# A two-layer AdaLN/FFN kernel: c turned by VectorE in 32x32 blocks, conv moved in front of up's second half

## What is computed

```python
# layer 0
att = softmax(mlp(cond))                                   # (b, 8)
y   = einsum('boi,bih->boh', einsum('bk,koi->boi', att, weight), x) + (att @ bias_k)[:, :, None]
x1  = x + y @ W_up.T + lora_B[e] @ (lora_A[e] @ y) * 1.0   # e = argmax(y @ gate_w.T + expert_bias)
# layer 1
c   = conv1d(x1, weight, 9 taps, pad 4, 4 groups) + (cond @ c_weight.T)[:, :, None] + bias
r   = route(softmax(c @ W_gate.T), top 2, renormalised)    # (tokens, 8 experts)
out = x1 + c @ W_base.T + b_base + einsum('bner,eor->bno', (c @ A.T) * r, B)
```

## Time and profile before

| | before |
|---|---|
| median of 3 runs | 400.89 us (400.55 to 401.44) |
| the profiled execution | 400.67 us |
| its span, first to last instruction | 398.9 us |
| mean granted TensorE clock | 0.996 |
| TensorE busy | 383.5 us, 96% |
| VectorE busy | 270.0 us, 68% |
| ScalarE busy | 103.5 us, 26% |
| GpSimd busy | 160.4 us, 40% |

### The profile page before, as it was taken

How to read it: one execution, slowest core, us unless ns; L and a number is a source line. 1 busy time by engine, 2 the same in 40 slices (tenths; PEclk the granted TensorE clock), 3 DMA queues, 4 the chain that set the end, 5 groups by cost and what they waited for, 6 DMA issues and landing times.

```text
span 398.9 us, 8234 instructions
## 1 busy us (share of the span) xinstructions
PE 383.5 (96%) x2615; PEld 354.9 (89%) x2615; DVE 270.0 (68%) x837; ACT 103.5 (26%) x251; POOL 160.4 (40%) x146
## 2 busy tenths in 40 slices
PE   4999999999999999999999999999999999999995
PEld 2887999989999999999999999999999999999984
DVE  4568667657766676777667767676677676766553
ACT  4733222222122222221222222212222222222211
POOL 4314444243444443334444433344444333444420
PEclk9989999999999999999999999999999999999999
DMA  5803342212122222112222321222222212222111
GB/s 131 268 15 114 116 140 81 80 32 65 64 78 79 79 79 74 37 61 65 79 79 79 79 78 30 63 66 79 79 79 79 58 50 64 66 79 79 54 53 55
DMA packets 31404, 30.75 MB, mean 77 GB/s; under 512 B 4740, under 2 KB 21556, under 8 KB 31392
## 3 DMA queue, kind: packets, MB, share of 16 engines
q1 hardware_dynamic: 31184, 30.19, 26.1%
q0 software_dynamic: 208, 0.41, 0.4%
HBM read 13.79 MB, written 8.40 MB: 56 GB/s over the span
## 4 chain that ended last, share of the span: by engine, by line
PE 86%; issue 2%; DVE 1%; DMA 1%; ACT 1%; SPq 0%; DVEq 0%
PE ps_base L912 18%; PE ps_conv L865 17%; PE ps_up L829 15%; PE ps_base L917 9%; PE ps_up L834 7%; PE ps_mix L789 7%; PE ps_base L883 5%; PE ps_ct L894 4%; PE ps_up L776 2%; PE ps_turn L768 2%; DMA xq<-x1p 1%; PE ps_turn L760 1%; SPq L293 0%; DVE x1p L598 0%; DVE c L680 0%
## 5 line engine op out<-in xcount | busy, mean ns | idle before, releaser
L364 POOL TENSOR_TENSOR y_lo<-y,y_hi 128x512 fp32r<-128x512 f32 x31 | 40.1, 1293 | 198.8 <-ACT y_hi L407 198.8
L912 PE MATMUL ps_base<-base_hi,c_hi 128*128 128x392 f32 (+1 forms) x256 | 77.7, 320 | 1.1 <-ACT c_hi L458 1.1
L912 PE MATMUL ps_base<-base_lo,c_hi 128*128 128x392 f32 (+1 forms) x256 | 75.0, 310 | 0.0
L829 PE MATMUL ps_up<-up_hi,y_hi 128*128 128x292 f32 (+1 forms) x256 | 67.9, 292 | 0.7 <-ACT y_hi L407 0.7
L829 PE MATMUL ps_up<-up_lo,y_hi 128*128 128x292 f32 (+1 forms) x256 | 67.5, 291 | 0.0
L508 DVE TENSOR_TENSOR mix_w<-gsum,quad 128x64 f32<-128x64 f32 x64 | 48.1, 753 | 6.6 <-DVE gl L648 5.3
L371 POOL TENSOR_TENSOR x1b<-x1p,bbase_s 128x512 f32<-128x512 f32 x32 | 50.1, 1566 | 4.1 <-DVE ot L688 4.1
L912 PEld LDWEIGHTS ps_base<-base_hi,c_hi 128*128 128x128 f32 x256 | 48.4, 189 | 1.5 <-DVE ot L688 1.5
L829 PEld LDWEIGHTS ps_up<-up_hi,y_hi 128*128 128x128 f32 x256 | 48.9, 191 | 0.9 <-ACT y_hi L407 0.9
L829 PEld LDWEIGHTS ps_up<-up_lo,y_hi 128*128 128x128 f32 x256 | 48.9, 191 | 0.0
L917 PE MATMUL ps_base<-base_hi,c_lo 128*128 128x392 f32 (+1 forms) x256 | 48.4, 311 | 0.0
(11 more groups left out here) (156 smaller groups left out, 626.7 us busy)
## 6 DMA issues: line engine op xcount, KB each, us to landing
xt<-in_x SPq DMA_DIRECT2D x32, 256.0 KB, 3.0
xq<-x1p SPq DMA_DIRECT2D x128, 64.0 KB, 2.2
out_x<-ot SPq DMA_DIRECT2D x32, 256.0 KB, 3.0
rows<-agg_rows SPq DMA_DIRECT2D x2, 597.0 KB, 4.1
wup_raw<-in_L_ffn_W_up SPq DMA_DIRECT2D x2, 512.0 KB, 5.5
wbase_raw<-in_L_ffn_W_base SPq DMA_DIRECT2D x2, 512.0 KB, 5.2
rows<-agg_rows SPq DMA_DIRECT2D x1, 598.0 KB, 4.7
rows<-agg_rows SPq DMA_DIRECT2D x1, 256.0 KB, 4.0
```

What stands on the lines that cost most here:

```text
L364: pool.tensor_tensor(y_lo[:], y32[:], y_hi[:], ALU.subtract).then_inc(ylo_done, 1)
L829: pe.matmul(into, y_hi[:, k], w[:, k, cols], start=(k == 0 and w is up_hi), stop=False, skip_group_check=True)
L912: pe.matmul(ps_base[:, j, 0:width], c_hi[:, q], w[:, q, j, 0:width], start=(q == 0 and w is base_hi), stop=False, skip_group_check=True)
```

## The change

- c of tile i-1 is evicted from PSUM by ScalarE, one activation (Identity, with the bias as a per-partition operand) for each of the four samples, in place of two adds on VectorE.
- It is turned by two VectorE instructions of 128x256 that transpose 32x32 blocks, SBUF to PSUM, in place of four TensorE transposes. The partitions of the turned c are then (phase, low five bits of the position), so w_base, a1 and w_gate are reordered to match, by GpSimd copies ahead of the fills; w_gate's fill becomes the last one.
- TensorE's order in a middle step becomes: up with the gate's columns, conv's first six products, the turn of hw, conv's last three, up's other columns with the turn of z before its last four products, delta, LoRA product, mix, base.
- On VectorE the output sum is split in two halves of 256 columns, one on either side of x1p; base waits for its own half only.
- Of x1's four transfers SP issues two; ScalarE issues the other two, after c_hi and before y_high of the next tile.

The diff, cut to its core:

```diff
+        base_p, a1_p, g1_p = sb("base_p", [P, KC, H]), sb("a1_p", [P, H]), sb("g1_p", [E1, H])
 ...
-            fills.append(((in_base, 32), [wbase_raw[:, dc, q:H:NQ] for dc in range(KC)], KC, P,
+            fills.append(((basep_ready, KC), [base_p[:, dc, cols] for dc in range(KC)], KC, P,
 ...
@@ sync
-                    for b in range(SPT):
+                    for b in range(SPT // 2):
                         sp.dma_start(xq[:, b, 1:1 + NM], x1p[b * C:(b + 1) * C]).then_inc(xq_in, 16)
@@ gpsimd, before the steps
+            pool.wait_ge(in_base[0], 16)
+            for dc in range(KC // 2):
+                pool.tensor_copy(by_chunk(base_p[:, dc]), chunk_rows(wbase_raw[:, dc])).then_inc(basep_ready, 1)
             pool.wait_ge(y32_done, 1)
             pool.wait_ge(yhi_done, 1)
             pool.tensor_tensor(y_lo[:], y32[:], y_hi[:], ALU.subtract).then_inc(ylo_done, 1)
+            pool.wait_ge(in_base[1], 16)
+            for dc in range(KC // 2, KC):
+                pool.tensor_copy(by_chunk(base_p[:, dc]), chunk_rows(wbase_raw[:, dc])).then_inc(basep_ready, 1)
+            pool.wait_ge(in_a1, 16)
+            pool.tensor_copy(by_chunk(a1_p[:]), chunk_rows(a1_raw[:])).then_inc(a1p_ready, 1)
+            pool.wait_ge(in_gate, 16)
+            pool.tensor_copy(by_chunk(g1_p[:]), chunk_rows(g1_raw[:])).then_inc(g1p_ready, 1)
@@ scalar
+            def conv_out(t):
+
+                act.wait_ge(conv_done, t + 1)
+                after(act, ct_done, t * 2)
+                for b in range(SPT):
+                    act.activation(c32[:, b], ps_conv[:, 0, b * NM:(b + 1) * NM], ACT.Identity,
+                                   bias=biasT[:, bass.ds(t * SPT + b, 1)]).then_inc(c32_done, 1)
 ...
+                if final:
+                    z_high(i)
+                if once(i - 1):
+                    conv_out(i - 1)
 ...
+                if once(i) and not final:
+                    z_high(i)
 ...
-                    act.wait_ge(ct_done, i)
+                    act.wait_ge(ct_done, i * 2)
 ...
+                if once(i):
+
+                    act.wait_ge(x1_done, i + 1)
+                    after(act, xqlo_done, i)
+                    for b in range(SPT // 2, SPT):
+                        act.dma_start(xq[:, b, 1:1 + NM], x1p[b * C:(b + 1) * C]).then_inc(xq_in, 16)
                 if once(i + 1):
                     y_high(i + 1)
@@ vector
+            def turn_c(t):
+
+                after(dve, clo_done, t)
+                for half in range(2):
+                    dve.wait_ge(c32_done, t * SPT + (half + 1) * (SPT // 2))
+                    dve.transpose(ps_ct[:, 0, half * HALF:(half + 1) * HALF],
+                                  c32[:, half * (SPT // 2):(half + 1) * (SPT // 2)].rearrange("p b m -> p (b m)"))\
+                        .then_inc(ct_done, 1)
+
+            def out_sum(i, par, j):
+
+                if j == 0:
+                    dve.wait_ge(delta_done, i - 1)
+                    dve.wait_ge(x1b_done, i - 1)
+                    after(dve, stored[par], pair_count(i, par, -4))
+                dve.tensor_tensor(ot[:, par, j * HALF:(j + 1) * HALF], ps_base[:, j, 0:HALF],
+                                  x1b[:, par, j * HALF:(j + 1) * HALF], ALU.add).then_inc(out_done, 1)
 ...
                 if final:
+                    z_low(i)
                     x1_sum(i, par)
                 if once(i - 1):
-                    dve.wait_ge(conv_done, i)
-                    after(dve, ct_done, i - 1)
-                    for half in range(2):
-                        b2 = slice(half * SPT // 2, (half + 1) * SPT // 2)
-                        dve.tensor_tensor(c32[:, b2], ps_conv[:, 0].rearrange("p (b m) -> p b m", b=SPT)[:, b2],
-                                          biasT[:, bass.ds((i - 1) * SPT + half * (SPT // 2), SPT // 2)].unsqueeze(2)
-                                          .to_broadcast([P, SPT // 2, NM]), ALU.add).then_inc(c32_done, 1)
+                    turn_c(i - 1)
+                if once(i) and not final:
+                    z_low(i)
                 if once(i - 2):
-                    dve.tensor_tensor(ot[:, par].rearrange("p (j d) -> p j d", j=2), ps_base[:, :, 0:HALF],
-                                      x1b[:, par].rearrange("p (j d) -> p j d", j=2), ALU.add)\
-                        .then_inc(out_done, 1)
+                    out_sum(i, par, 0)
                 if once(i) and not final:
                     x1_sum(i, par)
+                if once(i - 2):
+                    out_sum(i, par, 1)
@@ tensor
+            def up_half(t, j, cols, done, between=None):
 ...
+                if j == 1:
+                    pe.wait_ge(ylo_done, t + 1)
+                if between is not None:
+                    between(t)
 ...
                     pe.wait_ge(yhi_done, i + 1)
                     after(pe, x1_done, i)
+                    up_half(i, 1, slice(HALF, L0W), upgate_done)
+                if once(i) and (final or not once(i - 1)):
+                    up_half(i, 0, slice(0, HALF), up_done)
 ...
                     pe.wait_ge(xqhi_done, i)
-                    after(pe, c32_done, (i - 1) * 2)
+                    after(pe, c32_done, (i - 1) * SPT)
                     for part, (rhs, weights) in enumerate(((xq_hi, (conv_hi, conv_lo)), (xq_lo, (conv_hi,)))):
                         if part == 1:
-                            if last:
+                            if once(i - 2) and not final:
                                 turn_hw(i - 2)
                             if final:
                                 lora_delta(i)
-                            elif once(i):
-                                turn_z(i)
                             pe.wait_ge(xqlo_done, i)
 ...
+                elif once(i) and not final:
+                    up_half(i, 0, slice(0, HALF), up_done, turn_z)
 ...
-                    after(pe, clo_done, i - 1)
-                    for b in range(SPT):
-                        if b % (SPT // 2) == 0:
-                            pe.wait_ge(c32_done, (i - 1) * 2 + 1 + b // (SPT // 2))
-                        mm = pe.transpose(ps_ct[:, 0, b * P:(b + 1) * P], c32[:, b], ident[:])
-                    mm.then_inc(ct_done, 1)
 ...
-                    after(pe, out_done, i - 1)
                     for j, width, done in ((0, L1W, basegate_done), (1, HALF, base_done)):
+                        after(pe, out_done, (i - 2) * 2 + 1 + j)
```

More of the change, by code:

```diff
@@ L369, in body @@
                     pool.wait_ge(x1_done, i + 1)
-                    after(pool, out_done, i - 1)
+                    after(pool, out_done, (i - 1) * 2)
                     pool.tensor_tensor(x1b[:, par].rearrange("p (m q) -> p m q", q=NQ),
@@ L575, in _ @@
             y_sum(0)
-            for n in range(3, NF0):
+            for n in range(3, NF1):
                 low_part(n)
@@ L754, in _ @@
                 .then_inc(attb_done, 1)
+            def up_half(t, j, cols, done, between=None):
+                into = ps_up[:, j, 0:cols.stop - cols.start]
+                for k in range(KC):
+                    for w in (up_hi, up_lo):
+                        pe.matmul(into, y_hi[:, k], w[:, k, cols], start=(k == 0 and w is up_hi),
+                                  stop=False, skip_group_check=True)
+                if j == 1:
+                    pe.wait_ge(ylo_done, t + 1)
+                if between is not None:
+                    between(t)
+                for k in range(KC):
+                    mm = pe.matmul(into, y_lo[:, k], up_hi[:, k, cols], start=False,
+                                   stop=(k == KC - 1), skip_group_check=True)
+                mm.then_inc(done, 1)
             def turn_hw(t):
@@ L818, in body @@
             def body(i, par):
+                final = isinstance(i, int) and i == NT - 1
+                last = isinstance(i, int) and i >= NT
                 if once(i):
@@ L822, in body @@
                     after(pe, x1_done, i)
-                    for j, cols, done in ((1, slice(HALF, L0W), upgate_done), (0, slice(0, HALF), up_done)):
-                        into = ps_up[:, j, 0:cols.stop - cols.start]
-                        for k in range(KC):
-                            for w in (up_hi, up_lo):
-                                pe.matmul(into, y_hi[:, k], w[:, k, cols], start=(k == 0 and w is up_hi),
-                                          stop=False, skip_group_check=True)
-                        if j == 1:
-                            pe.wait_ge(ylo_done, i + 1)
-                        for k in range(KC):
-                            mm = pe.matmul(into, y_lo[:, k], up_hi[:, k, cols], start=False,
-                                           stop=(k == KC - 1), skip_group_check=True)
-                        mm.then_inc(done, 1)
+                    up_half(i, 1, slice(HALF, L0W), upgate_done)
+                if once(i) and (final or not once(i - 1)):
+                    up_half(i, 0, slice(0, HALF), up_done)
```

(4 more changed lines are left out.)

56 lines of the change are left out of this document (27 added, 29 removed).

## The result

| | before | after |
|---|---|---|
| median of 13 runs each | 400.19 us (398.64 to 402.14) | 403.54 us (401.25 to 405.14) |
| ratio, 95% interval | | 1.0077 (1.0054 to 1.0101) |
| the profiled execution, its span | 400.67, 398.9 us | 402.86, 401.0 us |
| mean granted clock | 0.996 | 0.996 |
| tile: mean distance of delta's first products, 60 to 340 us | 11.45 us | 11.467 us |

The account below looks back on a forecast made before the run. TensorE's stream was taken as the bound, with about 0.3 us a tile of waits. 29 tiles of 11.0 against 331.57 gave -12.6, start 0, end +0.5: span 386.8, so 388.8 us as median; range 379 to 399.

Parts of the forecast that it names:

- a loop over the output sum, x1p, c_lo, y_hi and GpSimd to conv: Loop setting the tile: 10.96 us by c_lo's arm, 11.04 by GpSimd's; taken as 11.0 against 11.43.
- x1p starts at D+0.54: On VectorE: the first half sum waits until D+0.19, takes 0.35, then x1p starts.
- That chain just fits.: c's evictions, VectorE's transposes and z_low end at about S+2.95, when TensorE wants z_low at the LoRA product.
- The second rival: c's new chain too slow: output sum 0.4 to 0.5 later, tile 11.4, gain gone, 400 us; chance 0.13.
- The third rival: ScalarE's transfer issues hold y_hi up 0.94 if both queues slow each other; tile 11.98, 417 us; chance 0.11.
- S to D: TensorE from conv's last three products to delta's end: 0.83 + 1.41 + 0.71 = 2.95 us.
- the floor: TensorE's stream without waits, 10.64 us a tile; as a rival, c_lo and xq_lo on time, 378.4; chance 0.12.
- 0.32 late: c_lo usable at D+2.60 where TensorE wants to load it at D+2.28, in each tile.
- costed at nothing: mix_w makes zm late, but z's turn moves 0.94 us back in TensorE's stream, so no cost was expected.
- Needed: Splitting x1's transfers over two queues lets xq_hi start near D+4.5; worth 0 to 0.1 us a tile.
- The start: Fills and GpSimd weight copies ahead of the middle tiles: sum 0, bounds -1.5 to +1.5 us.
- The end: Tiles 30 and 31, where conv feeds base directly, plus the split last sum: +0.6; tile 31 keeps -0.1.

Follow-up runs that it names:

- e2: The changed kernel with GpSimd making xq_lo before x1b; 401.43 us, ratio 1.0034.
- e6: The changed kernel with all four of x1's transfers issued by SP; 400.80 us, ratio 1.0026.
- e12: The changed kernel with xq_lo before x1b, c_lo before the second half sum, z_low between c's transposes, quad in PSUM, 14 identity transposes before the last base; 381.96 us.
- e8: The kernel before with mix_w's constant operand quad kept in PSUM; 394.86 us, ratio 0.9869.
- e9: The kernel before with three of c's four TensorE transposes left out in each tile; 399.29 us, ratio 0.9982.
- e11: The changed kernel with mix_w's constant operand quad kept in PSUM; 401.53 us, ratio 1.0040.
- e7: The changed kernel with xq_lo before x1b, c_lo before the second half sum, and all four transfers on SP; 409.50 us, ratio 1.0237.
- e4: The changed kernel with both swaps: xq_lo before x1b, and c_lo before the output sum's second half; 390.84 us, ratio 0.9782.
- e1: The changed kernel with four transposes of c put back on TensorE as idle work, result unused; 405.45 us, ratio 1.0138.
- e5: The changed kernel with 14 extra transposes of the identity on TensorE before the last base; 402.34 us, ratio 1.0067.
- e3: The changed kernel with VectorE making c_lo before the output sum's second half; 402.97 us, ratio 1.0102.
- e2 with quad: The changed kernel with xq_lo before x1b and mix_w's operand quad in PSUM; 394.52 us, ratio 0.9868.

## Why the prediction was wrong

The mechanism was named as it is: a loop over the output sum, x1p, c_lo, y_hi and GpSimd to conv, with waits for c_lo and xq_lo in its wake. **Its length was wrong, 11.04 for 11.47, and that is the whole forecast gain of 0.39 a tile.** Means over 23 tiles, from D (0.71 behind delta's first product); S is the start of conv's last three products:

| | forecast | measured |
|---|---|---|
| output sum's first half starts | D+0.19 | D+0.33 |
| x1p starts | D+0.54 | D+0.82 |
| c_lo starts | D+1.87 | D+2.14 |
| y_hi starts | D+3.19 | D+3.52 |
| y_lo, x1b, xq_lo behind it | 0.78, 1.24, 1.53 | 0.78, 1.25, 1.51 |
| xq_lo usable (S) | D+8.09 | D+8.42 |
| S to the next D | 2.95 | 3.05 |

- **x1p, the step that failed: 0.28 of the 0.43.** "x1p starts at D+0.54" was made of D+0.19 for the first half sum and 0.35 behind it. The half sum's wait for delta ends at D+0.17, as costed, but the sum begins at D+0.20 in every other tile and at about D+0.43 in the rest (the tile shown is one: 208.93), D+0.33 on the mean, with x1p 0.34 to 0.40 behind it: D+0.70, as e2 has it. In the late ones a register instruction of VectorE's sequencer stands behind the wait; that it is the cause isn't shown. The other 0.12 is the LoRA product. x1p reads ps_up and waits for it, 0.20 behind the product's end; in e2 that end is D+0.41, here D+0.61, because the product itself waits for z_low.
- **"That chain just fits."** It does not: z_low ends at S+3.10 on the mean (in the tile shown at 208.57, S+3.13), for S+2.95. The evictions came out in sum as costed: the first starts S+1.15, 0.16 later than the sum needs, but 369 ns each and 0.27 apart they end at S+2.29, as forecast (of the four ends listed there only this last one fits a start at S+0.99 and 0.40 each; the others are one eviction's starts). The transposes start 0.03 behind the second and fourth eviction and take 459 ns, inside their bounds and beyond the 0.36 taken: S+2.79 for S+2.70. z_low adds 0.31 for 0.25. The groups of after:

```profile
L433 ACT ACTIVATE c<-ps_conv,biasT 128x128 f32<-128x128 f32 x128 | 36.6, 369 | 29.8 <-PE ps_conv L913 29.8
L651 DVE STREAM_TRANSPOSE ps_ct<-c 128x256 f32<-128x256 f32 x64 | 29.2, 459 | 15.4 <-ACT c L433 13.8
```

  The Trainium skill's figure weighed there ("VectorE: DVE Perf Modes", The three transpose paths; it is for bf16) would by estimate have given 0.62 a transpose; the trace, 0.459 in float32, lies between that and the 0.36 to 0.42 taken, nearer the latter. The same page's advice (Rules for kernel authors: TensorE where PSUM may be the destination) came out right, but the transposes' length is only about a tenth of a microsecond of the 0.43.
- **The second rival, in part.** Its sign of being wrong did appear: the LoRA product waits for z_low. But not at its price and not by its way: the output sum is held by delta, not by the transposes.
- **y_hi, 0.06 more.** ScalarE's two issues take 1.49 us on the mean, 0.73 each. In the tile shown they end at 211.93, 0.11 ahead of y_hi: hidden by 0.1, not 0.3. The profile puts y_hi's wait down to y; and still e6 shows y_hi 0.08 earlier without them. The third rival (two queues that slow each other) needed 0.77 an issue. SP's two, beside ScalarE's, take 0.6 each as before; why ScalarE's are longer isn't shown.
- **S to D, 0.10 more.** e12 has the same leg, 3.03, with no wait in it. So it is stream: up's second half with z's turn among its products takes 1.54 (206.25 to 207.79), 0.13 more than the 1.41 without. Among conv's products the turn had cost 0.04. e12's tile without any wait is 10.77, where the floor was put at 10.64.
- **c_lo: right, but by two errors that cancel.** 0.32 late was forecast and 0.27 measured. It is loaded at D+2.87, for D+2.60; and TensorE wants it at D+2.60, for D+2.28, because the LoRA product has held it up as well (mix starts at D+0.45; D+0.24 in e12). **xq_lo**: 0.08 forecast, 0.37 measured; the errors above end in this wait.
- **What comes off the kernel before.** Its stream is 11.25 (e8, no wait for zm left), so zm's wait was worth 0.2 a tile of 11.43 to 11.45, where "about 0.3" had been said. And e9 shows that the four turns were no pure gain even there.
- **mix_w, costed at nothing: right in the middle of this kernel (e11), and only there.** e2 and e7 meet it, the kernel before paid 5.2 us for it, and the start of e6, below, pays too.
- **The split transfers.** "Needed", worth 0 to 0.1 a tile: in this kernel they cost 0.05, and with the loop loosened they are worth 0.7 (e7 against e4).
- **The start** was forecast 0 with 1.5 either way, and is 0.3 earlier in after. Two things move it from one execution to the next. One is the clock. e1's start is the same code, and its tile 2 is 1.4 later. The stretch from 20 to 26 us (columns as above), first after, then e1:

```profile
20.00:26.00 6.00, 4.94 (x41) 4.57 (x39) 5.40 (x15) 2.99 (x7) 6.00 (x7) 1.00 0.12 32
20.00:26.00 6.00, 6.00 (x40) 5.94 (x39) 4.28 (x13) 1.89 (x4) 6.00 (x7) 0.72 0.14 31
```

  Of the changed kernel's family e1, e7 and e12 have a stretch of half clock there, and tile 2's LoRA product at 49.13 to 49.96; seven of the eight without it have it at 47.96 to 48.76. The eighth, e6, shows the other: mix_w and the *new* GpSimd copies. Its gate came 0.18 us later than in after, so that both halves of tile 1's mix_w lie behind copies. They take 1.07 and 1.51 us, for 0.45 and 0.97 in after, and z's turn waits for zm:

```profile
23.56 1.13 POOL L366 COPY g_p<-g_raw 8x512 f32<-8x512 f32 x1
23.81 1.51 DVE L541 TENSOR_TENSOR mix_w<-gsum,quad 128x64 f32<-128x64 f32 x1
25.97 0.29 PE L823 MATMUL ps_turn<-ident,zm 128*96 128x128 f32 x1 [1.39 <-DVE zm L709]
```

- **The end**, forecast +0.6, is +2.3 here, and +0.8 without the clock's fall: from tile 31's LoRA product to the end it takes 20.1 before, 22.4 after, 20.9 in e5 (378.49 to 399.4) and in e3. The sum was right, the fall not thought of.

Between the profiled executions 2.2 us were lost and between the medians 3.3. The other 1.1 is in no trace, but the timed executions give a hint: of after's thirteen, the seven with a mean granted clock of 0.987 to 0.992 have spans of 401.7 to 403.3 us, the six with 0.996 to 1.000, the profiled one among them, 399.4 to 401.0. Why the changed kernel should have the lower clock more often isn't shown.

The range (379 to 399) was too narrow for the same reason: the rivals each took one price wrong. That several legs of one loop are all a tenth or two longer than their best reading, with nothing in the loop to absorb it, wasn't among them.

## What to carry to other kernels

When work is taken off the busiest engine, time the loop that the new order closes: each leg by what it *waits* for rather than by what stands before it in the old trace, and by its mean over tiles rather than by one tile. In the old order some of those waits were covered. If a loop comes within a few tenths of the engine's stream, the order on the idle engines (GpSimd's, VectorE's) can be worth more than the edit: here two swaps turned +0.8% into -2.2%, and neither alone shortened the tile by more than 0.02 us. And an instruction that is long for its size, as mix_w, may be waiting inside for another engine. It is worth finding out first, since any reordering can move it on or off the path.

## What the runs showed of the hardware

- A GpSimd operation under way holds up a VectorE product with both operands in SBUF: mix_w takes 0.22 to 0.23 us when it starts first or has one operand in PSUM, and up to 1.64 (e2) when it starts behind; it then ends 0.08 to 0.09 us behind a GpSimd operation's end in nearly all cases. "SBUF — State Buffer", Who interferes with whom (the Trainium skill), states it as an exclusive lock on the port pair that the two engines share, for a VectorE instruction with two SBUF inputs and a GpSimd one that reads SBUF, with the issue order deciding who blocks; the traces agree, 0.04 us of order deciding over 1.2 us. The other half of that rule, GpSimd held up by VectorE, is hardly seen: the 28 x1b that start inside a mix_w in e4 take 1.57 us on the mean and 1.62 at most, the other four 1.55.
- TensorE's granted clock fell from 1.00 to 0.50 (2.4 to 1.2 GHz) 0.1 to 1.5 us after its products had begun again behind 1.78 us idle, in four profiled runs (after, e1, e2, e7). The same products were not slowed behind 1.77 to 1.78 us in three others (e3, e4, e6), nor behind 1.52 and 1.53 (e2 with quad, e11), 0.57 or 0.25.
- A 128x128 turn on TensorE costs it about 0.12 us in a row of them (e5: 14 in 1.69), while 128x256 of 32x32 blocks hold VectorE 0.46 us: per column TensorE's is about half.
